# A GNN kernel on Trainium2: the bias of the MLP's output moves from a matmul on TensorE to an add on GpSimd

## The reference, cut to what matters

```
y = cond_layer_norm(x, cond, s1, b1)
x = x + (softmax attention over the edges, 4 heads)(y) @ wo + bo
y = cond_layer_norm(x, cond, s2, b2)
x = x + relu(y @ m_w1 + m_b1) @ m_w2 + m_b2
```

## Time and profile before

| | |
|---|---|
| median of 3 runs | 1954.78 us (1954.19 to 1955.04) |
| the profiled execution's own time | 1956.64 us |
| its span in the profile | 1954.8 us |
| PE busy | 1783.7 us, 91% |
| DVE busy | 1306.0 us, 67% |
| ACT busy | 916.6 us, 47% |
| POOL busy | 423.4 us, 22% |
| mean granted clock of TensorE | 0.97 of full speed |

### The profile page before, as it was taken

One profiled execution on the slowest core, in us unless ns is written; L12 is line 12 of the kernel. 1 busy time (PEld: TensorE's weight loads), 2 busy tenths in 40 slices (PEclk: granted clock), 3 DMA queues, 4 the chain that ended last, 5 costly groups with the idle time before them and its releaser, 6 DMA issues.

```text
span 1954.8 us, 31300 instructions
## 1 busy us (share of the span) xinstructions
PE 1783.7 (91%) x11879; PEld 1527.7 (78%) x11879; DVE 1306.0 (67%) x2411; ACT 916.6 (47%) x1471; POOL 423.4 (22%) x499
## 2 busy tenths in 40 slices
PE   3447579999999999999999999999999999999898
PEld 3446557888888788888887888888878888888777
DVE  8997785676685655766856567668565676585744
ACT  6557664454454244544542445445424454453221
POOL 5562223000025230000251300002513000024300
PEclk9678789999999999999999999999999999999999
DMA  3020155242231022422410224223102233232122
GB/s 117 11 49 10 57 223 186 85 148 90 85 127 50 16 83 81 142 90 85 133 44 16 88 84 135 96 83 129 44 16 90 76 131 104 88 115 86 40 69 76
DMA packets 63635, 170.06 MB, mean 87 GB/s; under 512 B 5857, under 2 KB 24066, under 8 KB 63485
## 3 DMA queue, kind: packets, MB, share of 16 engines
q10 hardware_dynamic: 23040, 102.41, 15.6%
q1 hardware_dynamic: 40452, 65.69, 10.3%
HBM read 146.58 MB, written 17.02 MB: 84 GB/s over the span
## 4 chain that ended last, share of the span: by engine, by line
PE 75%; DVE 10%; issue 7%; ACT 3%; DMA 2%; DVEq 2%; SPq 1%; POOL 1%; POOLq 0%; ACTq 0%
PE ps L1442 65%; PE ps L1654 8%; DVE onehot L1032 1%; PE ps L1574 1%; DVE prob L1198 1%; DVE PT_lo L1214 1%; DVEq L1056 1%; DVE CW L1068 1%; ACT PT_hi L842 1%; DVE CW L1071 1%; DVE CW L1064 1%; DMA piece<-in_L_gnn_m_w_dram 1%; PE ps L1869 1%; DVE CW L1066 0%; SPq L388 0%
## 5 line engine op out<-in xcount | busy, mean ns | idle before, releaser
L842 ACT ACTIVATE PT_hi<-ps 128x512 fp32r<-128x512 f32 x400 | 238.5, 596 | 245.0 <-PE ps L1654 244.1
L1214 DVE TENSOR_TENSOR PT_lo<-ps,PT_hi 128x512 fp32r<-128x512 f32 x400 | 274.1, 686 | 50.0 <-ACT PT_hi L842 42.4
L826 ACT ACTIVATE prob<-prob,nmax 128x1250 f32<-128x1250 f32 x160 | 214.0, 1338 | 139.0 <-DVE nmax L1198 139.0
L1654 PE MATMUL ps<-ident,prob 128*128 128x128 f32 x1600 | 248.4, 278 | 11.9 <-DVE PT_lo L1214 11.9
L1198 DVE CUSTOM_DVE_ANT_0 prob<-ps,Lr 128x1250 f32<-128x1250 f32 x160 | 232.2, 1451 | 33.6 <-PE ps L1442 32.2
L1654 PEld LDWEIGHTS ps<-ident,prob 128*128 128x128 f32 x1600 | 181.7, 140 | 78.8 <-DVE PT_lo L1214 61.1
L1442 PE MATMUL ps<-PT_hi,v_hi 128*128 128x256 f32 x800 | 228.0, 285 | 1.1 <-DVE PT_lo L1214 1.1
L1442 PE MATMUL ps<-PT_lo,v_hi 128*128 128x256 f32 x800 | 226.1, 283 | 0.0
L1442 PE MATMUL ps<-PT_hi,v_lo 128*128 128x256 f32 x800 | 225.9, 282 | 0.0
L1442 PE MATMUL ps<-yT,wqk_hi 128*128 128x512 f32 (+1 forms) x768 | 213.0, 364 | 4.3 <-DVE yT L1151 4.3
L1442 PE MATMUL ps<-win,onehot 128*128 128x112 bf16 x1680 | 113.8, 240 | 101.0 <-DVE CW L1071 78.3
(11 more groups left out here) (205 smaller groups left out, 3797.5 us busy)
## 6 DMA issues: line engine op xcount, KB each, us to landing
Lr<-l_table ACTq DMA_DIRECT2D x160, 625.0 KB, 3.9
piece<-in_L_gnn_m_w_dram SPq DMA_DIRECT2D x32, 256.0 KB, 2.7
w_table<-CW SPq DMA_DIRECT2D x5, 1250.0 KB, 7.5
l_table<-CW SPq DMA_DIRECT2D x10, 625.0 KB, 3.2
prob<-w_table SPq DMA_DIRECT2D x10, 625.0 KB, 3.9
x<-in_x_dram SPq DMA_DIRECT2D x2, 2304.0 KB
CW<-CW SPq DMA_DIRECT2D x7, 625.0 KB, 5.8
piece<-in_L_gnn_wv_dram SPq DMA_DIRECT2D x16, 256.0 KB, 2.7
```

The costliest lines, as they stand in the source:

```text
L826: act.activation(buf, buf, ACT.Exp, bias=nmax[:, i % 4:i % 4 + 1], scale=-1.0, accum_out=rsum[:, i % 4:i % 4 + 1]).then_inc(S["exped"], 1)
L842: act.activation(o, i, ACT.Copy).then_inc(S["pt_hi"], 1)
L1214: dve.tensor_tensor(lo, i, hi.bitcast(F32), ALU.subtract).then_inc(S["pt_split"], 1)
L1654: m = pe.transpose(bank(5 + n % 2, at * P, (at + 1) * P), prob[:, (NT * h + 2 * g + j) % 3, d * P:(d + 1) * P], ident[:])
```

## The change

TensorE's bias matmul at the head of each `mlp_out(t)` is gone; the first of the twelve passes now starts the accumulation. GpSimd has a new `add_b2(t)`, which adds `bo_rows` to tile t of x once VectorE has read the tile for the second norm; two of them stand at the head of each pair c. For this SP loads `m_b2` of the layer into the buffer `bo_rows` (`load_b2`) once all ten `add_bo` are done, and `bo` of the next layer into it (`load_bo`) once all ten `add_b2` are done. VectorE's `add_mlp(t)` waits for `b2_added` besides `m2_ready`. The blocks of `bo` and `m_b2` leave `stacks`, `b_stack` and `row_raw`: two row loads and one third of a layer's `stacks2_in` DMAs fall away, the DRAM write of `b_stack` has 5 rows in place of 7, and two of GpSimd's memsets over `stacks` are 512 elements shorter.

```diff
-S1, S2, B1, B2, BV, BO, MB2 = range(7)
-KINDS, CKINDS = 7, 4
+S1, S2, B1, B2, BV = range(5)
+KINDS, CKINDS = 5, 4
...
-            for k, name in enumerate(("s1_b", "s2_b", "b1_b", "b2_b", "bv", "bo", "m_b2")):
+            for k, name in enumerate(("s1_b", "s2_b", "b1_b", "b2_b", "bv")):
...
+            def load_b2(l):
+                sp.wait_ge(S["bo_added"], START + l * PER["bo_added"] + NT)
+                sp.dma_start(bo_rows[:], T["L0_gnn_m_b2"][bass.ds(l, 1), :].broadcast_to([P, D])).then_inc(b2_in, 16)
...
             def layer(l, ahead):
                 sp.wait_ge(S["m2_ready"], START + l * NT)
                 load_stacks(l, slice(S2, CKINDS, 2), slice(S2, CKINDS, 2), stacks2_in)
-                sp.dma_start(stacks[SLOTS * C16:SLOTS * C16 + 3, MB2_AT:MB2_AT + 1, :],
-                             b_stack[:, MB2:KINDS, bass.ds(l, 1), :].rearrange("i k o d -> i k (o d)")).then_inc(stacks2_in, 16)
                 for n in range(AHEAD_PIECES, AHEAD_PIECES + 2):
                     load_piece(l, n)
                 if ahead:
                     sp.wait_ge(S["v_ready"], START + l * PER["v_ready"] + NT)
-                    sp.wait_ge(S["bo_added"], START + l * PER["bo_added"] + NT)
                     start_rows(l + 1)
-                    load_bo(l + 1)
+                load_b2(l)
                 for n in range(AHEAD_PIECES + 2, PER["piece_split"]):
                     load_piece(l, n)
                 if ahead:
                     for n in range(AHEAD_PIECES):
                         load_piece(l + 1, n)
+                    sp.wait_ge(S["b2_added"], START + l * PER["b2_added"] + NT)
+                    load_bo(l + 1)
...
-                pool.memset(stacks[0:SLOTS * C16, CKINDS:KINDS - 1, :], 0.0).then_inc(stack_set, 1)
+                pool.memset(stacks[0:SLOTS * C16, CKINDS:KINDS, :], 0.0).then_inc(stack_set, 1)
...
-                pool.memset(stacks[SLOTS * C16:STACK, S2 + 1:KINDS - 1, :], 0.0).then_inc(stack_set, 1)
+                pool.memset(stacks[SLOTS * C16:STACK, S2 + 1:KINDS, :], 0.0).then_inc(stack_set, 1)
...
+                def add_b2(t):
+                    wait("centered", NT + t + 1)
+                    pool.tensor_tensor(x[:, t, :], x[:, t, :], bo_rows[:], ALU.add).then_inc(S["b2_added"], 1)
...
+                pool.wait_ge(b2_in, l * 16 + 16)
                 for c in range(GROUPS):
+                    add_b2(2 * c)
+                    add_b2(2 * c + 1)
                     h_rest(c, 0)
                     h_rest(c, 1)
...
                 def add_mlp(t):
                     wait("m2_ready", t + 1)
+                    wait("b2_added", t + 1)
...
                     o = bank(4 + 3 * j)
-                    mm(o, cstack[:, nt(t)], stacks[:, MB2_AT, :], True, False)
                     for k in range(KT):
                         m = mm3(o, hT_hi[:, c % 2, k, nt(j)], hT_lo[:, c % 2, k, nt(j)], mw_hi[1][:, k, :], mw_lo[1][:, k, :],
-                                False, k == KT - 1)
+                                k == 0, k == KT - 1)
...
-                pe.wait_ge(stacks2_in, l * 16 * 3 + 16 * 3)
+                pe.wait_ge(stacks2_in, l * 16 * 2 + 16 * 2)
```

More of the change, by code:

```diff
@@ L58 @@
 STACK = SLOTS * C16 + 4
-MB2_AT = 5
 AHEAD_PIECES = KT + 2
-S1, S2, B1, B2, BV, BO, MB2 = range(7)
-KINDS, CKINDS = 7, 4
+S1, S2, B1, B2, BV = range(5)
+KINDS, CKINDS = 5, 4
 BIAS_ROWS = 3 * LAYERS * KT
@@ L124 @@
     o_ready=H * GROUPS, o_part=2, o_hi=H * GROUPS, o_split=H * GROUPS,
-    wo_ready=H * NT, x_added=H * NT, bo_added=NT,
+    wo_ready=H * NT, x_added=H * NT, bo_added=NT, b2_added=NT,
     bn_done=2 * NT, centered=2 * NT, inverted=H * NT, var_eps=2 * NT, h_ready=2 * GROUPS, h_relu=2 * GROUPS, h_split=2 * GROUPS,
@@ L149, in build @@
         cstack = sb("cstack", [STACK, NP], BF16)
-        stacks = sb("stacks_sb", [STACK, KINDS - 1, D], BF16)
+        stacks = sb("stacks_sb", [STACK, KINDS, D], BF16)
         bias_all = sb("bias_all", [P, 3, LAYERS, KT], F32)
@@ L276, in build @@
         piece_in = [sem(f"piece_in{i}") for i in range(2)]
-        stacks1_in, stacks2_in, bo_in = sem("stacks1_in"), sem("stacks2_in"), sem("bo_in")
+        stacks1_in, stacks2_in, bo_in, b2_in = sem("stacks1_in"), sem("stacks2_in"), sem("bo_in"), sem("b2_in")
         noise_in, f_in, bias_in, x_in, src_in, weight_in, dst_in = (
```

## The result

The changed kernel takes 1946.52 us in the median of 5 runs (1944.94 to 1947.58) against 1955.04 for the kernel before in the same rounds (1954.19 to 1958.67): a ratio of 0.9952 with a 95% interval of 0.9937 to 0.9967, thus 8.5 us less, where 10.4 were forecast. Timed again later, it was 1946.25 against 1955.61, ratio 0.9955 (0.9942 to 0.9968). The profiled execution took 1946.52 us with a span of 1944.5, 10.3 us less than the span before. That this equals the forecast to a tenth turned out to be luck: two of its terms are not borne out, and a stretch taken as unchanged moved. The experiments show which. Both medians, 1946.52 and 1946.25, lie in the stated range of 1941.5 to 1948.2, but just above the main case's own range, which ended at 1946.0.

A forecast was written before the change was run, and what follows sets the result against it. The prediction took TensorE's instruction stream to bound the MLP. Gains of 9.2 (bias matmuls), 0.9 (preparation) and 0.3 us (DMA) sum to 10.4, from the median 1954.78 to 1944.4 us, range 1941.5 to 1948.2.

The forecast's parts named there:

- main case: Whole kernel: the summed gains all arrive, 1944.4 us, own range 1943.0 to 1946.0; chance 79%.
- TensorE's stream bounds the MLP: MLP: each of 40 removed bias matmuls shortens the kernel by 0.23 us, 9.2 us in all (8.8 to 9.6).
- The end of a layer holds: End of a layer's MLP: VectorE falls slightly behind TensorE, but 4.3 us ahead of the next layer's transposes hold it; no loss.
- a new wait eats part of it: Rival, end of a layer: bound by VectorE, 12 bias matmuls pay nothing, 2.8 us lost, 1947.2 us; chance 6%.
- GpSimd's adds are covered: MLP pairs: 40 adds, 51.4 us, 2.57 per pair, fit GpSimd's idle time (11.2 of 11.7 us in the fullest); cost nothing.
- GpSimd becomes the bound: Rival, MLP: binds from 2.4 us per add; at 3.6 us, 3.8 us per layer, 1965.1 us in all; chance 4%.
- VectorE is not held by the adds: MLP: VectorE's norm (734 to 748 ns) and output add (656 to 693) keep their times beside GpSimd; cost nothing.
- The moved loads cost nothing: SP queue: loading m_b2 where bo was, 15 us free, and bo after the last add_b2 costs nothing.
- The preparation, 0.9 us: Before the layers: two shorter GpSimd memsets save 0.86 us, and VectorE's one-hots gain 0.9 us (0 to 1.3).
- the preparation moves by a whole GpSimd instruction: Rival, preparation: one one-hot more or less held by a 3.6 us instruction, 1948.0 or 1940.8 us; chance 8%.
- The third stacks DMA, 0.3 us: First scores: they wait 0.88 us for the third stacks DMA; removing it gains a third, 0.3 us (0 to 0.88).
- The last stage: Behind the last layer: taken as unchanged, with no term in the sum.

The follow-up runs named there:

- matmuls out: The kernel before without its 40 bias matmuls and with nothing in their place: 1946.81 us against 1956.20, ratio 0.9948.
- adds beside: The kernel before with the change's GpSimd adds, loads and waits, bias matmuls kept: 1956.06 us, ratio 1.0002.
- the two kernels with repeated adds: The changed kernel with every GpSimd add of m_b2 done twice or three times: 1950.88 us (0.9975 to before) and 2005.02 us (1.0254).
- three adds: The changed kernel with every GpSimd add of m_b2 done three times: 2005.02 us, ratio to before 1.0254.

## Why the prediction was right, point by point

- **TensorE's stream bounds the MLP.** Shown by matmuls out: the same 68.5 us without any adds. Forecast 9.2 us (8.8 to 9.6), measured 9.0 in the profiles. The intervals of the times are too wide to tell 9.0 from 10.4. The price was 0.23 and is 0.22 in layers 0 to 2, 0.24 in the last.
- **The end of a layer holds.** Shown: the stretch from the first value matmul to the next scores is 43.98 us in every kernel, and no wait at the transposes. The rival "a new wait eats part of it" did not occur.
- **GpSimd's adds are covered.** Shown for the MLP by adds beside (70.74 us, ratio 1.0002) and by the two kernels with repeated adds, which find the edge near the forecast 2.4 us per tile. What the forecast did not have is the 0.6 to 0.7 us in the third heads of layers 2 and 3. Of the rival "GpSimd becomes the bound" the size of the add from which it binds was right. The price was not, and the place in part (the first waits are at the last pair): for an add of 3.6 us it had 3.8 us per layer, and three adds of 1.29 (3.9 us) cost 16. The steps that were missing are the end of the MLP and the granted clock.
- **VectorE is not held by the adds.** 690 to 693 and 733 to 749 ns: right.
- **The moved loads cost nothing.** Shown by adds beside, which has them all.
- **The preparation, 0.9 us.** The local part is right: memsets 0.58 and 1.72 us, the next GpSimd instructions 0.86 earlier. That it stays until the layers begin is not shown: the first profiles had 2.4 us, and repeated profiles of one program differ by more. Matmuls out, with the preparation of before, is as fast as the changed kernel. The rival "the preparation moves by a whole GpSimd instruction" is not an alternative to the main case but its everyday spread, from one execution to the next; the range should have had it as noise of some 3 us. Against it the forecast had held that VectorE is tied to GpSimd's chain; the four lines above show a one-hot come before GpSimd's instruction in one execution and behind it in another.
- **The third stacks DMA, 0.3 us.** Wrong. The wait of the earlier trace rows was 0.88 us, and 0.83 in the second profile of before; in three profiles of the changed kernel it is 0.81, 0.61 and 1.08 (timeline of PE, first profile):

```profile
310.88 0.50 PE L1452 MATMUL ps<-k_hi,q_hi 128*128 128x512 f32 x1 [0.81 <-DMA stacks_sb<-b_stack]
```

  Over all profiles the wait ends 8.4 to 8.8 us after the issue of the first of these DMAs in the four with three of them, and 8.2 to 8.9 us in the ten with two, so the third cost nothing. That the loads queued ahead of them set the time is likely, but not shown.
- **The last stage** was taken as unchanged. It was 130.84 and 131.06 us in the two profiles of before, and 131.3 to 132.2 in all ten of the other table rows. Windows over its first 36 us, of the kernel before and of the changed one:

```profile
1823.96:1860.00 36.04, 30.87 (x146) 24.51 (x145) 32.39 (x61) 11.09 (x20) 9.21 (x22) 0.91 0.14 54
1812.64:1848.70 36.06, 30.89 (x142) 24.35 (x141) 31.76 (x61) 11.10 (x20) 9.44 (x22) 0.86 0.15 54
```

  The granted clock is 0.91 before and 0.86 after, thus some 6.5 and 10 us at 1.2 GHz, where TensorE waits 2.2 and 2.0 us for `lw_lo` in both kernels; adds beside, with all the matmuls of before, has 0.86 and 132.06 too, and matmuls out, without any add, 0.86 and 131.94. So neither the adds nor the missing matmuls are needed for it. It is 0.91 in the second profile of before as well. The third profile of the changed kernel has 0.86 too and only 131.3 us, so the clock is not all of it. What decides it stays open; in the changed kernel it takes back 0.3 to 1 us.

So the sum of 10.4 was met by the span's 10.3 with 9.0 from the MLP, 2.5 from a preparation that happened to be short, 0.2 lost in the stretches of attention and 1.0 in the last stage. The mechanism of the 9.2 was right; that the rest came out at the forecast's 1.2 in these two profiles was luck. The medians' 8.5 and 9.4 are what the MLP gives, within their intervals.

## What to carry to other kernels

Where one engine's stream is dense and nothing waits behind it, a removed instruction is worth its start-to-start distance, and moving work to an idle engine is free, or nearly so (0.6 us outside the MLP here), up to the slack of the fullest repeat of the loop: sum that repeat's busy time, compare it with the loop's pace, and also look at the last repeat, where no later one absorbs the lateness. Beyond that edge the price is not the excess alone: with three adds TensorE's granted clock fell behind its waits, too. Take a small term of a sum seriously only if the stretch it lies in repeats to better than that term: here the MLPs repeat within some 0.1 us and the preparation within 6.

## What the runs showed of the hardware that was not expected

- The same preparation, in the same program, reached the first scores between 306.69 and 312.55 us in three executions, while each of the later stages repeated within 0.1 to 1 us. That is 0.3% of the kernel's time in spread; runs of the kernel before went from 1950.61 to 1957.03 us within one set of rounds.
- A bf16 matmul costs 0.25 us between the float32 passes of the last layer, where six of the ten follow such a pass directly, and 0.22 on average in the other layers, where in the first layer three of ten do.
- With TensorE waiting for GpSimd, the granted clock in a stretch of 9.85 us of the MLP was 0.68 in place of 1.00: behind a wait of 5.7 us the first twelve passes ran at 1.2 GHz.
